# The order of an attention prologue's products, seventeen rough pairs in it, and one copy two slots later

## What is computed

```python
x = x + xattn(layernorm(x), ctx, Wq, Wk, Wv, Wo, bo)      # touched
x = x + ffn(layernorm(x), router_w, w1, b1, w2, b2)       # not touched
...
q = (x @ Wq).reshape(B, Nq, h, dh)          # x: 2048 x 256, h = 16, dh = 64
k = (context @ Wk).reshape(B, Nk, h, dh)    # context: 1601 x 192
v = (context @ Wv).reshape(B, Nk, h, dh)
attn = softmax(einsum('bqhd,bkhd->bhqk', q, k) / sqrt(dh))
out = einsum('bhqk,bkhd->bqhd', attn, v).reshape(B, Nq, h * dh)
return out @ Wo + bo
```

## Time and profile before

| | us |
|---|---|
| median of 3 runs | 1433.66 |
| the 3 runs | 1431.53, 1433.66, 1433.77 |
| the profiled execution, its own time | 1441.22 |
| its span in the profile | 1439.4 |
| PE busy in the span | 1314.9 (91%) |
| DVE, ACT, POOL busy | 1028.2, 792.8, 901.0 |
| mean granted clock of PE | 0.958 |

### The profile page before, as it was taken

One profiled execution on the slowest core, in us unless ns is written; L12 is line 12 of the kernel. 1 busy time (PEld: TensorE's weight loads), 2 busy tenths in 40 slices (PEclk: granted clock), 3 DMA queues, 4 the chain that ended last, 5 costly groups with the idle time before them and its releaser, 6 DMA issues. The chain is left out here.

```text
span 1439.4 us, 25028 instructions
## 1 busy us (share of the span) xinstructions
PE 1314.9 (91%) x8354; PEld 830.2 (58%) x8354; DVE 1028.2 (71%) x1677; ACT 792.8 (55%) x1073; POOL 901.0 (63%) x459
## 2 busy tenths in 40 slices
PE   4889999999999999999999999999989715999995
PEld 3645555455555555555555555555439715999995
DVE  6567777777777778777777877877796574665552
ACT  2326666566666566666566666666554113656652
POOL 3306887786788688778768877868783003345453
PEclk8889999999999999999999999999999856999998
DMA  8260001001000100100010010011306232444422
GB/s 250 109 202 1 16 23 54 24 16 54 17 23 18 62 16 16 54 24 16 25 54 16 16 62 16 23 45 67 114 30 220 62 117 92 119 127 106 97 39 24
DMA packets 75492, 88.81 MB, mean 62 GB/s; under 512 B 10443, under 2 KB 55532, under 8 KB 75372
## 3 DMA queue, kind: packets, MB, share of 16 engines
q1 hardware_dynamic: 68588, 78.32, 16.6%
q0 software_dynamic: 6784, 8.94, 3.8%
HBM read 58.98 MB, written 27.99 MB: 60 GB/s over the span
## 5 line engine op out<-in xcount | busy, mean ns | idle before, releaser
L810 POOL TENSOR_TENSOR acc_p<-acc_p,x_in 128x1024 f32<-128x1024 f32 x192 | 489.6, 2550 | 129.1 <-ACT x_in L910 123.0
L94 DVE TENSOR_REDUCE mx_part<-ps_m 128x1 f32<-128x512 f32 x558 | 366.9, 685 | 184.1 <-PE ps_m L82 182.3
L910 ACT ACTIVATE x_in<-ps_s 128x1024 f32<-128x1024 f32 x384 | 379.4, 1023 | 98.8 <-PE ps_s L726 74.0
L738 PE MATMUL ps_o<-x_in,v 128*64 128x512 f32 x1664 | 406.2, 606 | 0.0
L715 PE MATMUL ps_s<-q,k 64*128 64x512 f32 x2496 | 384.3, 395 | 0.9 <-ACT x_in L910 0.9
L715 PEld LDWEIGHTS ps_s<-q,k 64*128 64x128 f32 x2496 | 273.3, 185 | 43.4 <-ACT x_in L910 6.6
L82 PE MATMUL ps_m<-k,q 64*128 64x512 f32 x744 | 217.8, 457 | 14.8 <-ACT kept L580 6.1
L738 PEld LDWEIGHTS ps_o<-x_in,v 128*64 128x64 f32 x1664 | 99.5, 136 | 179.6 <-issue 142.2
L82 PEld LDWEIGHTS ps_m<-k,q 64*128 64x128 f32 x744 | 102.1, 185 | 153.8 <-issue 98.0
L810 DVE TENSOR_TENSOR acc_d<-acc_d,x_in 128x1024 f32<-128x1024 f32 x96 | 167.7, 1747 | 5.9 <-ACT x_in L910 5.5
L94 DVE TENSOR_REDUCE mx_part<-kept 128x1 f32<-128x512 f32 x186 | 127.6, 686 | 24.8 <-ACT kept L580 22.8
(11 more groups left out here) (246 smaller groups left out, 1963.6 us busy)
## 6 DMA issues: line engine op xcount, KB each, us to landing
w_in<-in_w SPq DMA_DIRECT2D x16, 1024.0 KB, 5.0
v_st<-rec_scr SPq DMA_DIRECT2D x64, 128.0 KB, 2.9
o_scr<-v_st SPq DMA_DIRECT2D x32, 256.0 KB, 2.1
v_scr<-c_in SPq DMA_DIRECT2D x13, 512.0 KB, 2.6
v<-v_scr SPq DMA_DIRECT2D x8, 832.0 KB, 5.3
c<-o_scr SPq DMA_DIRECT2D x2, 1792.0 KB, 9.0
x_in<-in_x SPq DMA_DIRECT2D x4, 512.0 KB, 8.8
k<-o_scr SPq DMA_DIRECT2D x1, 2048.0 KB, 9.1
```

Source lines behind the costliest of these rows:

```text
L94: dve.tensor_reduce(part[:, j // S.MF, j % S.MF:j % S.MF + 1], bank[:, 0:S.MC], AX.X, ALU.max).then_inc(done or G.rough_used[hd], 1)
L738: last = pe.matmul(ps_o[hd * HP:hd * HP + DH, :], v[b][:, s, hd * DH:(hd + 1) * DH], probs[:, g % RING, hd * QC:(hd + 1) * QC], start=(s = ...
L810: eng.tensor_tensor(acc, other, probs[:, (u * KT + t) % RING, :], ALU.add).then_inc(done, 1)
L910: act.activation(probs[:, g % RING, :], ps_s[:, g % 2, :], ACT.Exp, bias=G.pad_bias[:, 0:1] if s == KT - 1 else 0.0, scale=SCALE).then_inc ...
```

## The change

In the prologue:

- wv gets its own buffer (`w_in2`) and is loaded right behind the context, ahead of wk, x and wq. The context comes in chunks of four tiles with a semaphore each.
- ACT makes the high parts of all weights (not DVE), in pieces: two halves of wv, then the first 128 columns of wk and the rest, then the same of wq. DVE makes the low part of wv's first half, POOL those of all other pieces.
- PE's list begins, after the context's turns, with values. Keys, x's turns and queries stand between value jobs. A table (`BANK_USE`) says in which order the four PSUM banks are used.
- ACT copies all 26 value halves; DVE none. A fourth slot for values lies in `acc_d`.
- The 17 first rough jobs (13 of unit 0, four of unit 1) run in the prologue, from the thirteenth value job on, and so do the reduction of unit 0's maxima, its transpose, the copy and the placing.
- The root's table is loaded at the start by a root of one column.

In the attention: what moved to the prologue is left out, counts are adapted, and `DIFF_HI`'s (1, 10) becomes (1, 12).

```diff
...
-        w_in = [G.v0[:].rearrange("p (k n) -> p k n", k=2), G.acc_p[:]]
-        w_in.append(w_in[0])
+        w_in = [G.v0[:].rearrange("p (k n) -> p k n", k=2), G.acc_p[:], sb("w_in2", [P, 2, S.DI])[:]]
...
-        vjobs = [(kt, half) for kt in range(KT) for half in range(2)]
+        vjobs = [(kt, half) for g in range(0, KT, 2) for half in range(2) for kt in range(g, min(g + 2, KT))]
...
+        BANK_USE = ("v0 v1 v2 v3 k0 k1 v4 k2 k3 v5 v6 v7 v8 v9 q0 v10 q1 v11 q2 v12 q3".split()
+                    + [f"v{n}" for n in range(13, len(vjobs))])
...
+                load_split(2, "wv")
                 load_split(0, "wk")
...
-                sp.wait_ge(s_wlo, 1)
-                load_split(2, "wv")
...
-                store_weight(0, G.wk_scr)
+                store_weight(0, G.wk_scr, K_LO)
...
+                low(2, half1, V_HI)
+                low(0, pair0, K0_HI)
+                low(0, pairs, K_HI)
+                low(1, pair0, Q0_HI)
+                pool.wait_ge(s_xn, TT)
+                low(1, pairs, Q_HI)
...
+                for j in range(NC):
+                    lo(j)
+                dve.wait_ge(s_whi, V_HI - 1)
+                dve.tensor_tensor(w_lo[2][:, :, half0], w_in[2][:, :, half0], raw(w_hi[2][:, :, half0]), ALU.subtract).then_inc(s_vlo, 1)
+                for g in range(3):
+                    stats_of(g)
+                for n in range(2):
+                    proj_lo(n)
+                stats_of(3)
...
+                def keep_v(n):
+                    kt, half = vjobs[n]
+                    act.wait_ge(s_v, n + 1)
+                    if kt >= VS:
+                        act.wait_ge(s_vst[kt % VS], 16 * (kt // VS))
+                    act.activation(v_slot[kt % VS][:, (half0, half1)[half]], bank(f"v{n}")[:], ACT.Copy).then_inc(s_vev, 1)
...
+                for n in range(5, 7):
+                    keep_v(n)
                 act.wait_ge(s_mv, TT)
-                act.wait_ge(s_eps, 1)
+                act.wait_ge(s_eps, 2)
                 act.activation(std[:], mv[:, :, 1], ACT.Sqrt, bias=eps[:, 0:1]).then_inc(s_std, 1)
...
+                keep_v(7)
+                weight_hi(1, pair0)
...
+                for g in range(4):
+                    turn(NC + 2 * g)
+                    turn(NC + 2 * g + 1)
+                    values(8 + g)
+                    if g >= 1:
+                        proj(NPJ + g - 1)
+                rough(0)
+                values(12)
+                proj(NPJ + 3)
+                rough(1)
+                for n in range(13, len(vjobs)):
+                    values(n)
+                    rough(n - 11)
+                pe.wait_ge(G.max_ready, 1)
+                pe.wait_ge(s_lo, NTJ)
+                pe.transpose(ps[2][0:2 * S.QT, 0:P], G.mx[:], ident[:]).then_inc(G.maxt_ready, 1)
+                for r in range(len(vjobs) - 11, MJOBS + MAHEAD):
+                    rough(r)
...
-DIFF_HI = ((1, 4), (1, 10), (2, 4), (2, 12))
+DIFF_HI = ((1, 4), (1, 12), (2, 4), (2, 12))
...
```

More of the change, by code:

```diff
@@ L87, in rough_scores, with place_mrow @@
     last.then_inc(G.rough_ready[hd], 1)
+def place_mrow(sp, S, G, buf):
+    half = P // 2
+    for hd in range(2):
+        sp.dma_start(raw(G.m_rows[hd * half:hd * half + 1, buf, :]), raw(G.m_row[hd * S.QT:(hd + 1) * S.QT, :])).then_inc(G.mrow_placed, 16)
 def rough_max(S, G, dve, bank, hd, j, done=None):
@@ new lines, in _ @@
+                weight_hi(2, half0)
+                for j in range(4, 6):
+                    hi(j)
+                weight_hi(2, half1)
+                for j in range(6, NC):
+                    hi(j)
+                keep_v(0)
+                weight_hi(0, pair0)
+                weight_hi(0, pairs)
+                for n in range(1, 4):
+                    keep_v(n)
+                proj_hi(0)
+                proj_hi(1)
+                keep_v(4)
+                proj_hi(2)
+                proj_hi(3)
@@ L392, in proj, with turn @@
                                  for k in range(KD)]
[L393 to L403 removed]
+                    bank_free(pe, proj_job(n))
+                    product(bank(proj_job(n))[:, 0:width(n)], terms).then_inc(s_proj, 1)
+                def turn(j):
+                    src, tiles, k = tjobs[j]
                     if j >= 4:
@@ new lines, in _ @@
+                pe.wait_ge(s_id, 2)
+                for j in range(NC):
+                    pe.wait_ge(s_c[j // 2], 64 if (j // 2 + 1) * 4 > KT - 1 and j // 2 * 4 < KT - 1 else 32)
+                    turn(j)
+                for n in range(4):
+                    values(n)
+                proj(0)
+                proj(1)
+                values(4)
+                proj(2)
+                proj(3)
+                for n in range(5, 8):
+                    values(n)
+                for g in range(4):
+                    turn(NC + 2 * g)
+                    turn(NC + 2 * g + 1)
+                    values(8 + g)
+                    if g >= 1:
+                        proj(NPJ + g - 1)
@@ L559, in used_count @@
                 return unit * MJOBS + j
-            read = j - sum(k < j for k in KEPT)
-            return MJOBS + (MJOBS - len(KEPT)) * (unit - 1) + read if not (isinstance(unit, int) and unit == 0) else j
+            return MJOBS + (MJOBS - len(KEPT)) * (unit - 1) + j - sum(k < j for k in KEPT) + sum(k < MAHEAD for k in KEPT)
         def pe_rough(pe, b, c, j, unit, heads=(0, 1)):
@@ L571, in kept_count @@
         def kept_count(j, unit):
-            return len(KEPT) * (unit - 1) + KEPT.index(j)
+            return len(KEPT) * (unit - 1) + KEPT.index(j) - sum(k < MAHEAD for k in KEPT)
         def act_rough(act, j, unit, count):
@@ L596, in dve_max @@
                 dve.wait_ge(rough_used[hd], used_count(unit, MJOBS, hd))
-            wait_for(dve, kept_read, len(KEPT) * unit)
+            dve.wait_ge(kept_read, len(KEPT) * unit - sum(k < MAHEAD for k in KEPT))
             wait_for(dve, maxt_ready, unit)
@@ L611, in sp_mrow @@
             sp.wait_ge(mrow_ready, unit + 1)
[L612 to L614 removed]
+            place_mrow(sp, S, G, u % 2)
         def proj_here(n, first, last):
```

266 lines of the change are left out of this document (130 added, 136 removed).

## The result

| | before | changed |
|---|---|---|
| time, median of 4 runs (us) | 1433.56 (1431.53 to 1433.77) | 1410.77 (1408.85 to 1411.23) |
| ratio, with its 95% interval | | 0.9842 (0.9825 to 0.9859) |
| profiled execution / its span (us) | 1441.22 / 1439.4 | 1411.23 / 1409.4 |
| first product of the list (us from the span's start) | 19.90 | 20.02 |
| copy of the last values begins | 90.58 | 80.92 |

The changed kernel is 1.6% faster. Of the 30.0 us between the two spans 5.4 are PE's busy time (1314.9 us before, 1309.5 now); the rest is time in which it stood still.

What follows compares the result with a forecast made beforehand. PE was taken as the bound, losing time to prologue pauses, the boundary and ACT's wait in unit 1. Gains of 13.1 and 9.5 sum to 22.6 us, from a median of 1433.66 to 1411.0, range 1405 to 1419.

Steps and rivals of the forecast that it cites:

- The copy: Attention, unit 1: copy two slots later removes ACT's wait for POOL's difference, 1.36 us per pair, 9.5 us in 7 pairs.
- The start: Prologue: first value product at 20.9 us, against a first product at 19.90 before; 1.0 us lost.
- The block: Prologue start: DVE's low half of wv waits until POOL's ends, 19.6, then takes 1.22; without the wait, start at 19.6.
- PE's work: Prologue: 46.0 us of jobs and turns, 10.6 of rough pairs; with start, pause and low clock the last value product at 83.5.
- The pause: Prologue, ahead of x's first turn: PE idles 3.0 us for root, refinement and four tiles; bounds 2.5 and 6.5.
- The boundary: Between last value product, 83.5, and attention's first value product, 94.0: DVE's reads end last, attention begins at 88.2.
- Prologue and boundary together: Up to the attention's first value product: at 94.0 instead of 107.1, a gain of 13.1 us.
- The fourth slot: Rival, prologue: value slot free too late, ACT waits 2 to 3 us at job 8; 1413.5 to 1414, chance 0.13.
- The pause of 6.5: Rival, prologue: values don't fill the pause ahead of x's turn; 3.5 us worse, 1414.5, chance 0.10.
- the slow clock: Rival, prologue: PE's granted clock stays at the lower level throughout; 1458 us, chance 0.04.
- only the listed 6.1 come: Rival, attention unit 1: the later copy gains just PE's listed waits, 6.1 us; 1414.4, chance 0.10.
- DVE and POOL don't collide: Rival, prologue: wv's halves run freely, pause 2.5, no second clock fall; 1408.2, everything better, chance 0.13.

Runs made afterwards that it cites:

- experiment 9: Changed kernel with POOL's low part of the second difference moved to unit 2's first tile, keeping at unit 2's slot 2: 1431.94 us, ratio 0.9883.
- experiment 2: Changed kernel with POOL's low part of wv's second half waiting until DVE has made the first half's: 1422.92 us, ratio 0.983.
- experiment 3: Changed kernel with ACT's root ahead of the copies of value jobs 5 to 7 instead of behind job 6: 1422.78 us, ratio 0.9826.
- experiment 1: The changed kernel run again with nothing altered: 1426.13 us, ratio 0.9856 to the kernel before.
- experiment 5: The kernel before with only the `DIFF_HI` entry (1, 10) as (1, 12): 1427.11 us, ratio 0.9959.

## Why the prediction was right, and where its steps were off

The median was put at 1411.0 and is 1410.8. The profiled execution was put at 1418.6 and is 1411.2: the 7.6 us by which the profile of before lay above its median were carried over as if they belonged to the kernel, and most of them were the waits for `h_f` in the experts (5.5 us listed). The 7.6 drop out of the forecast of the median, which is the old median less 22.6. Of the steps within that 22.6 several were off and cancelled, so that the median came within 0.2 us is in part luck.

- **The copy, 9.5 forecast, 7.8 measured.** The mechanism was right, and at the place itself it gave what unit 2 had shown, 6.53 to 5.15. What failed is "unit 2 shows the order without any added wait of PE": 0.28 per pair is given back two steps on, since DVE's sum now runs beside POOL's low part (2.12 against 1.21, removed in experiment 9). The lower bound, the 6.1 of listed waits, is passed by the traces (7.8 and 7.9): the rest was indeed in products spaced out.
- **The start, 20.9 forecast, 20.0 measured.** The block was right (2.65 against 1.23, experiment 2). wv landed 0.4 us earlier, and POOL's half began at 16.54 and not at 17.2.
- **PE's work, 83.5 forecast for its end, 80.9 measured.** The term that was mis-sized is the turns: 0.85 for four transposes, read from the earlier trace rows, is their length at the lower clock. The prediction said that they ran there at the lower clock and still took the same value for turns at full clock, where four take 0.40. That is 3.6 us for eight turns. The account of before closed all the same, because there the turns did run at the lower clock. Rough pairs took 0.71 beside a job and not 0.76, 0.7 less in fourteen. Against it, the lower clock cost more: 3.0 at the start (to 26 us) and 1.7 behind the pause, forecast 2.0 and 1.0. The prediction's argument that at full work the clock came back within 4 us in every stretch failed here: from the first product it took 6. With the start's 0.9, the pause's 0.2, 0.3 of waits for DVE and about 0.8 in handovers (a value job behind other work takes 1.24 to 1.27, not 1.15, eight times or so) this makes the 2.6.
- **The pause, 3.0 forecast, 2.79 measured**, with its cause, the root behind job 6's copy (experiment 3). Two of its terms were off and cancelled: from the root to the first L332 it is 1.46 us where 1.9 was put, and from there to the first turn of x 1.94 where 1.5 was put.
- **The boundary, 10.5 forecast, 10.7 measured** from the last value product to the attention's first. DVE's reads end last, as said; the first value product stands behind PE's own work at the lower clock, and in experiments 1 and 2 behind the load of the values by 0.32 and 0.45 us. The two ways are within half a microsecond, as the two equal sums of 5.8 had it.
- **Prologue and boundary together, 13.1 forecast, 15.5 measured**: 2.4 better. The copy is 1.7 worse. Two errors of opposite sign made the sum good; this was luck.
- **The rivals.** The fourth slot isn't late: ACT's copy of value job 8 runs at 42.09, and what it waited for is PE's product (1.49). The pause of 6.5 and the slow clock didn't come: the windows at the lower clock are those shown, and from 44 to 84 the clock is 1.00. That only the listed 6.1 come is excluded by the seven distances, and not by the times. Of the case "DVE and POOL don't collide" the opposite is shown.

What the forecast didn't hold is the last pair, 1.8 us worse in this trace, and a median that is 22.8 us better where the trace up to the last pair shows 20.7. If the kernel before as a rule has that fall of the clock too, as the kernel of experiment 5 had, the two agree; this was not shown.

## What to carry to other kernels

A duration read from a stretch at the lower clock isn't the price of the same work at full clock, even when an account of the old kernel closes with it: read each unit price beside the granted clock of its window, and if the change moves the work out of that stretch, halve what is bound by PE. When an edit takes 1.4 us of waiting from PE, look at what two other engines then do at the same time: work of theirs that lay apart may now meet, and part of the gain is given back by a block between DVE and POOL. And place an engine's step that waits for a slower engine behind the copies that PE needs, not ahead: taken away in unit 1 that wait was worth 1.1 us per pair, and put back in unit 2 it cost 1.6.

## What the runs showed of the hardware

- The clock behind the same start comes back at different times: the changed kernel's windows show 0.50 to 26 us in the first trace, and 0.95 in the window from 24 to 26 in experiment 1, with the first product at 20.02 and 20.64. The chip doesn't decide it: experiment 3, on the chip of experiment 1, shows 0.50 to 26 again, with the first product at 21.02. From the first product to the last value product the two traces of one kernel take 60.5 and 59.1 us, and this is where most of the difference is.
- Behind the pause of 2.79 us the clock fell in each of the 7 traces that had it, behind 0.61 in none of 3. In the last pair it fell behind the first pause of 1.8 us in 7 of the 12 traces, behind the second in one, and stayed in 4.
- Two vector subtractions on DVE and POOL that begin 0.8 us apart take turns: the second took 2.65 us against 1.23 alone, the first 2.34 against 2.38. It goes the other way round too: POOL's normalisation took 2.27 us when DVE's sum had begun 0.9 earlier (145.25 and 144.37), and 1.28 when it began ahead of DVE's.
- Chip 8 shows 5.8 to 8.6 us of PE's waits for ACT in the experts in all six traces, chip 1 none in four, with the same code there; the kernel before takes 1% longer on the first (1447.36 and 1448.73 against 1433.06). That the chip is the cause isn't shown: the first trace of the kernel before has 5.5 us of them, though its other runs take 1433, as on chip 1.
